# Joining the first norm and the first layer's convolution into one phase

## The reference

```
xn = (x - mean_c(x)) / sqrt(var_c(x) + eps)            # first norm, over the 48 channels
z  = einsum('bchw,dc->bdhw', xn, in_w) + in_b          # 48 -> 96 channels
z  = depthwise 3x3 convolution(z, dw_w) + dw_b
z  = z * sigmoid(z)                                    # SiLU
x_dbl = einsum('bkdl,ked->bkel', xs(z), x_proj)        # small projection, for the scan that follows
```

## Time and profile before

| | us |
|---|---|
| median of 3 runs | 1784.25 |
| lowest and highest | 1781.26, 1788.53 |
| profiled execution | 1779.62 |
| its span | 1777.8 |
| PE, DVE, ACT, POOL busy | 1357.8, 1287.9, 1137.2, 914.3 |

### The profile page before, as it was taken

The page is one execution under the profiler, slowest core; times in us unless marked ns, Lnnn a source line. Parts: engine busy times, 40 slices in busy tenths (PEclk is TensorE's granted clock), DMA queues, the critical chain, the costliest instruction groups (busy, mean ns, idle before and its releaser), DMA issues. The chain is left out here.

```text
span 1777.8 us, 16638 instructions
## 1 busy us (share of the span) xinstructions
PE 1357.8 (76%) x3950; PEld 512.2 (29%) x3950; DVE 1287.9 (72%) x1358; ACT 1137.2 (64%) x1768; POOL 914.3 (51%) x443
## 2 busy tenths in 40 slices
PE   4499947557475388883878888888889888774996
PEld 3333311101010277772212222222222222111785
DVE  1245529979799355552079999999999999993675
ACT  3423337758586156563778888888888888841554
POOL 4100005867869300000388888888888888870000
PEclk9799965555555599997878888888888889655998
DMA  5423331020200312221477777777777776633562
GB/s 133 113 73 101 102 114 47 2 95 0 85 12 1 101 53 77 79 63 46 112 178 177 168 176 173 175 175 175 174 175 169 175 174 160 153 80 73 128 165 70
DMA packets 137309, 200.04 MB, mean 113 GB/s; under 512 B 27387, under 2 KB 69629, under 8 KB 136450
## 3 DMA queue, kind: packets, MB, share of 16 engines
q1 hardware_dynamic: 135380, 196.53, 44.7%
q10 hardware_dynamic: 1854, 2.70, 0.6%
HBM read 145.55 MB, written 53.63 MB: 112 GB/s over the span
## 5 line engine op out<-in xcount | busy, mean ns | idle before, releaser
L1694 DVE TENSOR_TENSOR_SCAN m_h<-m_qa,m_state,m_ub 128x512 f32<-128x512 f32 x384 | 463.9, 1261 | 15.0 <-POOL m_ub L1306 10.7
L1306 POOL TENSOR_TENSOR m_ub<-m_dlb,m_bt 128x1536 f32<-128x1536 f32 x128 | 438.6, 3445 | 15.5 <-DVE m_h L1694 11.4
L1655 ACT ACTIVATE m_qa<-m_dlb,k_a 128x512 f32<-128x512 f32 x384 | 254.2, 682 | 89.4 <-DVE m_h L1694 88.1
L1065 POOL TENSOR_TENSOR b_u<-b_dl,b_z 128x1024 f32<-128x1024 f32 x48 | 126.0, 2626 | 236.8 <-DMA b_z<-scratch_z 188.5
L1508 PE MATMUL m_qc<-m_bcr,k_selc 32*128 32x512 f32 x256 | 165.3, 729 | 101.3 <-DVE m_g L1705 101.1
L1705 DVE TENSOR_TENSOR m_g<-m_h,m_qc 128x1536 f32<-128x1536 f32 x128 | 221.5, 1731 | 11.8 <-issue 6.6
L1525 PE MATMUL m_qy<-m_g,k_seld 128*32 128x512 f32 x768 | 175.1, 767 | 0.0
L902 PE MATMUL b_qb<-b_bc,k_pack_sel 96*128 96x512 bf16 x96 | 78.6, 819 | 109.1 <-DVE b_u L986 109.1
L960 ACT ACTIVATE b_qa<-b_dl,b_a 128x512 f32<-128x512 f32 x96 | 65.4, 684 | 92.5 <-DVE b_h L1001 74.5
L1285 POOL MEMSET m_cva<- 128x640 f32 x2 | 1.3, 632 | 234.5 <-POOLq L1910 234.5
L1451 PE MATMUL m_qf<-m_cva,k_conv 113*96 113x504 f32 (+1 forms) x192 | 107.1, 702 | 18.8 <-DMA m_cvb<-scratch_xpad 18.8
(11 more groups left out here) (178 smaller groups left out, 2763.7 us busy)
## 6 DMA issues: line engine op xcount, KB each, us to landing
m_dlb<-scratch_dldu SPq DMA_DIRECT2D x128, 384.0 KB, 10.2
m_bt<-scratch_brow SPq DMA_DIRECT2D x128, 256.0 KB, 5.9
scratch_dldu<-m_dldu SPq DMA_DIRECT2D x32, 384.0 KB, 3.2
scratch_z<-a_z SPq DMA_DIRECT2D x24, 256.0 KB, 4.7
b_z<-scratch_z SPq DMA_DIRECT2D x3, 2048.0 KB, 8.5
scratch_y<-b_yrow SPq DMA_DIRECT2D x12, 512.0 KB, 2.8
c_y<-scratch_y SPq DMA_DIRECT2D x16, 384.0 KB, 3.4
scratch_gate<-m_gt SPq DMA_DIRECT2D x32, 192.0 KB, 3.5
```

The costliest lines, as they stand in the source:

```text
L1065: nc.gpsimd.tensor_tensor(by_column(u[s][:], col), by_column(dl[s][:], col), seen(z[:], col, piece), ALU.mult).then_inc(u_ready, 1)
L1306: nc.gpsimd.tensor_tensor(ub[k % 3][:], dlb[u % 2][:, J:2 * J, :], bcast(bt[u % 2][:, n, :], J), ALU.mult).then_inc(ub_ready, 1)
L1655: nc.scalar.activation(q_a[:, j, :], dlb[u % 2][:, j, :], ACT.Exp, scale=G["a1"][:, j, n:n + 1]).then_inc(da, 1)
L1694: nc.vector.tensor_tensor_scan(h[k % 3][:, j, :], q_a[:, j, :], ub[k % 3][:, j, :], state[:, k % NS, j:j + 1], ALU.mult, ALU.add).then_inc ...
```

## The change

norm_phase and conv0_phase become one phase, front0_phase. Its programs are written out without hardware loops.

- Norm steps 0 to 4 (AHEAD = 5) come first, in the order of before. Steps 5 to 15 are placed in the units of the convolution: step 2i + 5 with the centre behind unit 0 of chunk i, step 2i + 6 behind unit 2. On PE the centre follows the projection of that unit and the variance that of the next; on ACT the square stands at the end of the unit and Ln and Exp at the end of the next, with a load of the Ln/Exp table set ahead of them and of the SiLU set behind them; on DVE the scale stands ahead of the taps two units on.
- SP's order is written out: four loads, the border stores, then for each step its store and the load four steps on; the rows of chunk 0 are loaded after the store of step 2, those of chunk 1 after step 4, those of chunk i + 2 inside chunk i once step 2i + 6 is stored.
- PSUM: step 4 and all later ones use slot 0; the banks of slots 1 to 3 are the convolution's. The classes Conv and Weights take their banks from these.
- The folding of the convolution weights (two DVE instructions) comes between step 4 and the loop (dve_conv), and waits for three loads that ACT now issues first. The rest of the preparation (pe_bias, act_alog behind one more table load, dve_make, the three weight stores) comes behind the last chunk.
- POOL's zero fills of the a_cv tiles come at the start.

The core of the diff:

```diff
+AHEAD = 5
+def front0_phase(nc, D, G, sems):
...
+        def slot(n):
+            return n % SLOTS if n < AHEAD else 0
+
+        def norm_at(u):
+
+            i, b = u // B, u % B
+            n = 2 * i + AHEAD + b // 2
+            return n if b % 2 == 0 and 0 <= u < UNITS and n < NCS else None
...
+            def load_rows(i):
+                s = i % 2
+                if i == 0:
+                    sp.wait_ge(zeroed, SLOTS + 2)
+                    sp.wait_ge(weights.stored, 16 * 3)
+                if i >= 2:
+                    sp.wait_ge(conv.pair_mm, done(B * (i - 2) + B - 1))
+                for n in range(0 if i == 0 else 2 * i + 1, min(2 * i + 3, NCS)):
+                    sp.wait_ge(xn_stored[n % SLOTS], 32 * (n // SLOTS + 1))
+                load_conv(sp, cv[s], D["xpad"], i, loaded[s])
...
+            for n in range(SLOTS):
+                load(n)
+            weights.sp_border(sp)
+            for n in range(AHEAD):
+                store(n)
+                if n == 2:
+                    load_rows(0)
+            load_rows(1)
+            for i in range(NCH):
+                store(2 * i + AHEAD)
+                store_bc(i - 1)
+                store(2 * i + AHEAD + 1)
+                if i + 2 < NCH:
+                    load_rows(i + 2)
+                store_z(i)
+            store_bc(NCH - 1)
+            weights.sp_store(sp)
...
+            for n in range(AHEAD + 1):
+                if n < AHEAD:
+                    centre(n)
+                if n > 0:
+                    var(n - 1)
+            for u in range(UNITS + 2):
+                if u < UNITS:
+                    convolve(u)
+                if u >= 2:
+                    project(u - 2)
+                if norm_at(u) is not None:
+                    centre(norm_at(u))
+                if norm_at(u - 1) is not None:
+                    var(norm_at(u - 1))
+            pe.wait_ge(left, done(NCH - 1))
+            pe.wait_ge(ready, NCS)
+            weights.pe_bias(pe)
...
+            act.preload_act_table_set(SILU_SET)
+            act.wait_ge(weights.early_loaded, 16 * len(weights.early))
+            for u in range(UNITS + 4):
+                if u < UNITS:
+                    conv.copy_low(act, u % B, u)
+                if 1 <= u <= UNITS:
+                    silu(u - 1)
+                if u >= 3 and (u - 3) % B == B - 1:
+                    split_hi((u - 3) // B)
+                if u >= 4 and (u - 4) % B == B - 1:
+                    split_mid((u - 4) // B)
+                if norm_at(u) is not None:
+                    norm.act_square(act, norm_at(u), 0)
+                if norm_at(u - 1) is not None:
+                    act.preload_act_table_set(LOG_EXP_SET)
+                    norm.act_rstd(act, norm_at(u - 1), 0)
+                    act.preload_act_table_set(SILU_SET)
+            act.preload_act_table_set(LOG_EXP_SET)
+            weights.act_alog(act)
...
+            for n in range(AHEAD):
+                scale(n)
+            weights.dve_conv(dve)
+            for u in range(UNITS + 4):
+                if norm_at(u - 2) is not None:
+                    scale(norm_at(u - 2))
+                if u < UNITS:
+                    taps(u)
...
+            weights.dve_make(dve)
```

More of the change, by code:

```diff
@@ L457, in stages_of @@
     return [(place[name][0], stage) for name, stage in sorted(stages.items(), key=lambda item: place[item[0]][1])]
[L460 to L538, removed]
@@ L652, in conv0_phase, with bank @@
         rest = [m.sb(f"a_rest{s}", [DI, CH]) for s in range(2)]
-        q = [m.ps(f"a_q{s}", [DI, CH]) for s in range(2)]
-        zeroed, act_z, proj, hi, left, mid, lo = (
-            m.sem(f"a_{n}") for n in ("zeroed", "act_z", "proj", "hi", "left", "mid", "lo"))
+        qn = [m.ps(f"n_q{s}", [P, 4, CS]) for s in range(SLOTS)]
+        def bank(s, half):
+            return qn[s][0:DI, 2 * half:2 * half + 2, :].rearrange("d a t -> d (a t)")
+        q = [bank(3, r) for r in range(2)]
+        norm = Norm(nc, m, G, "n", EPS6, qn, sq, rs)
@@ L663, in _ @@
             for s in range(2):
                 nc.gpsimd.memset(cv[s][:], 0.0).then_inc(zeroed, 1)
+            weights.pool_split(pool)
+            weights.pool_shape(pool)
         @block.sync
         def _(sp):
-            sp.wait_ge(zeroed, 2)
-            for s in range(2):
[L670 to L689, removed]
+            weights.sp_first(sp)
+            sp.wait_ge(zeroed, SLOTS)
+            def load(n):
+                if n >= NCS:
+                    return
+                s = n % SLOTS
+                if n >= SLOTS:
+                    sp.wait_ge(norm.centred, done(n - SLOTS))
+                load_x(sp, x[s], D["x"], n, x_loaded[s], CS)
@@ L693, in _, with centre @@
             conv.lead_pe(pe)
-            lead(pe, proj)
-            def convolve(i, s, b):
-                if b == 0:
-                    pe.wait_ge(loaded[s], dma_done(i, s, 32))
-                conv.products(pe, s, b, B * i + b)
-            def project(i, s, b):
+            lead(pe, proj, norm.centred)
+            pe.wait_ge(weights.consts, 16 * len(weights.first))
+            def centre(n):
+                pe.wait_ge(x_loaded[n % SLOTS], 32 * (n // SLOTS + 1))
+                if n >= SLOTS:
+                    pe.wait_ge(ready, n if n > SLOTS else 1)
+                norm.pe_centre(x[n % SLOTS], slot(n))
@@ new lines, in var, with convolve, project @@
+            def var(n):
+                norm.pe_var(pe, n, slot(n))
+            def convolve(u):
+                i, b = u // B, u % B
+                if u == 0:
+                    pe.wait_ge(ready, SLOTS)
+                    pe.wait_ge(weights.conv_made, 2)
+                if b == 0:
+                    pe.wait_ge(loaded[i % 2], 32 * (i // 2 + 1))
+                conv.products(pe, i % 2, b, u)
+            def project(u):
+                i, b = u // B, u % B
+                s = i % 2
@@ L731, in split_mid @@
-            def split_mid(i, s, b):
-                if b == B - 1:
-                    act.wait_ge(left, done(i))
-                    nc.scalar.activation(bc[s][:, 1, :], rest[s][:], ACT.Identity).then_inc(mid, 1)
-            over_pairs(act, B, 4, take((0, low), (1, silu), (3, split_hi), (4, split_mid)))
+            act.preload_act_table_set(LOG_EXP_SET)
+            lead(act, conv.low_out, act_z, hi, mid)
+            weights.act_load(act)
+            act.wait_ge(weights.consts, 16 * len(weights.first))
@@ new lines, in silu, with split_hi @@
+            def silu(u):
+                i, b = u // B, u % B
+                s = i % 2
+                if b == 0 and i >= 2:
+                    act.wait_ge(stored[s], nst * (i // 2))
+                act.wait_ge(conv.tapped, done(u))
+                nc.scalar.activation(z[s][:, b, :], conv.acc[b % 2][:], ACT.Silu, bias=G["l0_dwb"][:, 0:1]).then_inc(act_z, 1)
+            def split_hi(i):
+                if i >= 2:
+                    act.wait_ge(stored[i % 2], nst * (i // 2))
+                act.wait_ge(proj, done(i))
+                nc.scalar.activation(bc[i % 2][:, 0, :], q[i % 2], ACT.Identity).then_inc(hi, 1)
@@ new lines, in split_mid @@
+            def split_mid(i):
+                act.wait_ge(left, done(i))
+                nc.scalar.activation(bc[i % 2][:, 1, :], rest[i % 2][:], ACT.Identity).then_inc(mid, 1)
+            for n in range(AHEAD + 1):
+                if n < AHEAD:
+                    norm.act_square(act, n, slot(n))
+                if n > 0:
+                    norm.act_rstd(act, n - 1, slot(n - 1))
+            act.preload_act_table_set(SILU_SET)
+            act.wait_ge(weights.early_loaded, 16 * len(weights.early))
```

109 lines of the change are left out of this document (68 added, 41 removed).

## The result

The changed kernel takes 1763.66 us (median of 8 runs), the kernel before 1782.99 us (8 runs): ratio 0.9901, 95% interval 0.988 to 0.9922. That is faster by 1.0%; the forecast was 1765.4 and 1.06%. The profiled execution took 1764.51 us with a span of 1762.7.

The account below looks back on a forecast made before the run. PE was taken to bound the convolution stage, busy for all its 128.90 us. -41.5 + 19.0 + 3.6 = -18.9 us from a median of 1784.25 gave 1765.4 us, with an 8-in-10 range of 1757 to 1776.

Parts of the forecast that it names:

- start of the convolution: PE's first convolution matmul, at 44.6 instead of 86.08 since rows load after norm step 2: 41.5 us earlier.
- unit 0 longer than before, apart from its centre: First convolution unit on PE, taken as in the kernel before: no term in the sum.
- eleven norm steps on PE: Norm steps 5 to 15 in the convolution loop, 1.73 us each on PE: 19.0 us added, unit pairs 10.93 us.
- end of the phase: Setup work moved behind the last chunk and more semaphores: next phase 3.6 us later, bounds 2.8 and 4.4.
- sum at the scan's start: Start of the next phase, all terms together: 18.9 us earlier, near 226.6 instead of 245.46.
- ACT as the bound: Loop rival: costlier table switches make unit pairs 12 us, total 1777; 0.17 together with a start partly in the way.
- Late rows: Loop rival: row loads reach PE late and eat the gain; over 1779, 0.09 together with other stalls.
- The copy behind Ln and Exp: ACT's copy in the loop, free to start 2.9 us into the next unit, done at 3.5, not late for DVE.
- the larger rival: Larger gain: first units at the higher clock win about 2 us, earlier loading and shorter tail 2.5; about 1760, chance 0.12.
- a sign of being wrong: At the phase's end: a tail of over 8 us between the last store and the next phase.

Follow-up runs that it names:

- changed_again: The changed kernel itself, unaltered, measured and profiled a second time; 1761.76 us, ratio 0.9908 to the kernel before.
- tables_4: Changed kernel with two more activation table loads behind Exp in each of the 11 norm steps in the loop, four in all; one run, 1757.69 us.
- tables_6: Changed kernel with four more activation table loads behind Exp in each of the 11 norm steps in the loop, six in all; one run, 1792.82 us.
- rows_doubled: Changed kernel with an equal load into tiles nobody reads ahead of each row load from chunk 2 on; ratio 0.9907 to the kernel before.
- more_semaphores: Changed kernel with 30 more unused semaphores in the joined phase, 72 to clear instead of 42; one run, 1762.07 us.
- warm_pe: Changed kernel with 18 matmuls of constants on PE while it waits for the first rows; ratio 0.9884 to the kernel before.
- norm_first_setup_inside: Joined phase, all 16 norm steps first, chunk 0's rows loaded after step 11, setup work moved from the end to before unit 0; 1758.74 us, ratio 0.9886 to before.
- norm_first_late_rows: Joined phase, all 16 norm steps ahead of the convolution, rows of chunks 0 and 1 loaded only after step 15; one run, 1762.50 us.

## Why the prediction was right, step by step

| term | predicted | measured | second profile (changed_again) |
|---|---|---|---|
| start of the convolution | -41.5 | 44.87 - 86.08 = -41.2 | -41.3 |
| unit 0 longer than before, apart from its centre | 0 | 8.49 - 6.43 - 0.87 = +1.2 | -0.3 |
| eleven norm steps on PE | +19.0 | (208.82 - 53.36) - (229.80 - 92.51) + 0.87 = +19.0 | +19.0 |
| end of the phase | +3.6 | 8.15 - 3.70 = +4.45 | 8.06 - 3.70 = +4.4 |
| sum at the scan's start | -18.9 | -16.5 | -18.3 |

Read directly, the last row is 16.55 and 18.45; the rest is rounding and, in the second profile, 0.2 us between the last unit and the last store. (229.80 and 208.82 are the inner products of unit 31, 92.51 and 53.36 those of unit 1.)

The mechanism and three of the four terms stand. That the medians of the totals came within 2 us of the forecast is in part luck: they moved by 19.3 us, 1 to 3 more than the scan's start did in the two profiles, and behind the scan's start nothing was changed.

**The start.** The chain scale of step 2, store, landing, row load, matmul came to 44.6 and was 44.87. The load took 8.8 us instead of 8.1, within the bounds given, and was issued 0.4 earlier.

**The loop.** 10.93 was 10.94, and PE never waits. Of the rivals, ACT as the bound is refuted by tables_4, which gives it 2.6 us more in each pair at no cost; tables_6 shows that the mechanism exists and where it sets in. Late rows are refuted by rows_doubled. The copy behind Ln and Exp came as written, 115.44 - 112.67 = 2.8 us into the next unit where 2.9 was predicted, and DVE's taps waited for PE's product and not for the copy.

**Unit 0.** The prediction took unit 0 as in before and named a gain of 2 us from a warmer clock as the larger rival. No such gain came: PE began at the low clock after its 8.9 us of idling, as it had before after 19.8. What the zero missed is scatter. In the six profiles with this front (the changed kernel twice, rows_doubled, tables_4, tables_6, more_semaphores) unit 0 with its centre took 8.49, 6.97, 7.80, 6.93, 7.14 and 6.97 us, against 7.30 in the sum, so the zero was right on average and up to 1.2 us off in one profile. warm_pe shows that the clock is the cause: at 1.00 it takes 4.58. A bound for this term was missing.

**The end.** This is the term that was too small, 4.45 and 4.4 us where the bounds were 2.8 and 4.4. The stretch from the last store to the next phase, 8.15 and 8.06 us, is also over the 8 us that the prediction had named as a sign of being wrong (its own sum has 7.2). The sum hung the next phase on SP's last issue, 1.9 us behind the last store, and gave DVE's end, which it had 1.5 us later, no effect of its own. In fact SP issued its three stores in 1.24 us, the lower bound given, and DVE was last, 4.3 us behind the last store instead of the 3.4 worked out. From DVE's end to the next phase it was 3.86 us, and the sum leaves 3.8. The rest is PE's bias products and the wait for them: from 218.59 to 222.01, 3.4 us instead of the 2.8 of the earlier trace rows. The first group of them took 1.44 us instead of 0.83. Here is the granted clock in the changed kernel and in the kernel before:

```profile
218.50:221.00 2.50, 2.41 (x10) 2.23 (x11) 1.51 (x5) 2.36 (x4) 0.00 (x0) 0.50 0.94 233
```

```profile
63.50:64.40 0.90, 0.88 (x7) 0.86 (x8) 0.90 (x4) 0.22 (x2) 0.00 (x0) 0.94 0.55 147
```

At the seam of norm_first_setup_inside, at 1.00, the same group takes 0.72. So the low clock at the end costs the 0.6 us. Taking more for 42 semaphores than for 16 was right in size: 26 more at the measured 0.071 are 1.8 us, and the prediction had 5.3 - 3.7 = 1.6. The stretches of the earlier trace rows that it was read from depend on what ends last as well, since 25 semaphores took 5.1 there and 44 took 5.3.

**Where the gain came from.** The prediction said that norm work in the loop is not hidden, and the runs show it twice: one phase alone is worth 12.0 us, and the best order without interleaving has its scan as early as the changed kernel. What the change does buy is that no end of phase and no zero fill lie between the two stages, and that PE idles for 8.9 us ahead of the convolution instead of 19.8. It did not foresee that the norm steps of the joined phase would run at 2.1 us a step (the first scale at 27.35, the last at 58.94 in norm_first_late_rows) instead of 2.3 (27.65 and 62.78 before), which is 3.8 of those 12.0. SP's DMA pairs start 1.1 to 1.2 us apart in the kernel before (42.12, 43.29, 44.41) and 0.8 to 1.0 in that run (37.55, 38.39, 39.37, 40.31); that this is the reason was not tested.

## What to carry to other kernels

Work that is moved into a stage costs its full time on the engine that bounds that stage; here 19 of 41 us were paid back there and another 4.5 at the end. Before interleaving, try one phase with the stages still one after the other and the first loads of the next stage issued early, but behind the small loads that the current stage still needs: in one queue an 882 KB load in front cost 11 us. And look at the granted clock where PE has idled ahead of a stage or runs short of work at its end: here it cost 2.4 to 3.9 us in unit 0 and 0.6 at the end.

## What was not expected of the hardware

- Folding the convolution weights took DVE 3.71 us for two instructions, 0.45 for one and 3.34 for the other. It is so in all seven profiles where they stand at 38 us, and in each of them POOL runs a tensor_tensor of 3.25 to 3.27 us beside them (here from 38.44 to 41.70, and DVE ended at 42.02). In the kernel before and in the four programs with all norm steps first, where they come later, both take 0.45. Whether the two engines share a path is argued from this coincidence and not tested by moving POOL's instruction; here it cost nothing, as the rows came at 44.87.
- A table load costs ACT 1.28 to 1.29 us in a busy stream, with 0.02 us ahead of it and 0.01 behind (tables_4).
- Clearing a semaphore at a phase's end costs 0.071 us (more_semaphores).
- The same program took 8.49 us for unit 0 and its centre in one profile and 6.97 in another. In the first the granted clock was still 0.57 from 52 to 53, in the second it was already 1.00 from 50 to 51. So about 1.5 us of the difference between two profiles can lie here alone.
